# Relative attention: queries and keys loaded from GpSimd's queue, four places for raw rows, smaller groups of inverse roots at the end

## What is computed

```python
# first layer, per batch b and head h
srel = skew(einsum('bhnd,hmd->bhnm', qx, ex))          # row n moved by n places
qk   = (einsum('bhnd,bhmd->bhnm', qx, kx) + srel) / sqrt(8)
out  = softmax(qk - mask) @ vx ; x = layernorm(x + out @ Wp.T + bp)
# last layer, per token
y = sum over the two chosen experts of gate * gelu(h @ w1[e]) @ w2[e]
x = layernorm(x1 + y)
```

## Time and profile before

| | |
|---|---|
| median of 3 runs | 1973.78 us (1969.85 to 1980.45) |
| profiled execution | 1972.76 us, span 1971.0 us |
| busy share of the span | PE 87%, weight load 72%, DVE 70%, ACT 69%, POOL 50% |
| mean granted TensorE clock | 0.943 |
| attention of the first layer | from about 74 us to about 752 us |
| last layer's units, then the scatters that are left | to 1946 us, then to 1963.6 us |
| DMA | 349.7 MB, mean 177 GB/s; 1.54 MB in each quad's write and read |

### The profile page before, as it was taken

The page is one execution under the profiler, slowest core; times in us unless marked ns, Lnnn a source line. Parts: engine busy times, 40 slices in busy tenths (PEclk is TensorE's granted clock), DMA queues, the critical chain, the costliest instruction groups (busy, mean ns, idle before and its releaser), DMA issues. The chain is left out here.

```text
span 1971.0 us, 51107 instructions
## 1 busy us (share of the span) xinstructions
PE 1720.8 (87%) x15932; PEld 1410.7 (72%) x15932; DVE 1381.4 (70%) x5696; ACT 1368.5 (69%) x3385; POOL 978.2 (50%) x1256
## 2 busy tenths in 40 slices
PE   7799998999998998898999768898859999748994
PEld 6566665665655566788999758888748999727994
DVE  1388887887877785585432279999859888584663
ACT  3589988888888883423455458888849888515784
POOL 2133333333333333215667666666328989925755
PEclk9899999999999997999999979999979999857997
DMA  7899999999999994104566612222131212266852
GB/s 218 278 319 325 339 322 317 319 317 314 335 310 301 322 308 129 44 1 129 173 185 200 171 36 58 62 60 64 41 83 33 55 33 60 38 103 186 245 182 81
DMA packets 220349, 349.72 MB, mean 177 GB/s; under 512 B 55960, under 2 KB 167832, under 8 KB 219576
## 3 DMA queue, kind: packets, MB, share of 16 engines
q1 hardware_dynamic: 185096, 304.95, 48.9%
q0 software_dynamic: 14144, 31.16, 6.6%
q10 hardware_dynamic: 20848, 10.36, 1.8%
HBM read 160.52 MB, written 144.38 MB: 155 GB/s over the span
## 5 line engine op out<-in xcount | busy, mean ns | idle before, releaser
L184 POOL TENSOR_SCALAR_AFFINE_SELECT heads_raw_relative<-heads_raw_relative 128x508 f32<-128x508 f32 x256 | 158.8, 645 | 485.5 <-ACT heads_raw_relative L569 446.2
L575 ACT ACTIVATE attend_prob_t<-attend_turn_bank 128x384 f32<-128x384 f32 x512 | 225.3, 492 | 35.8 <-PE attend_turn_bank L493 34.5
L569 ACT COPY heads_raw_relative<-heads_rel_bank 128x768 f32<-128x768 f32 x247 | 198.0, 802 | 63.7 <-PE heads_rel_bank L464 30.9
L493 PE MATMUL attend_turn_bank<-ident,attend_score 128*128 128x128 f32 x1536 | 229.6, 285 | 5.4 <-ACT attend_prob_t L575 4.3
L493 PEld LDWEIGHTS attend_turn_bank<-ident,attend_score 128*128 128x128 f32 x1536 | 165.3, 142 | 94.4 <-ACT attend_prob_t L575 47.2
L628 DVE CUSTOM_DVE_ANT_0 attend_score<-attend_score_bank,heads_relative 128x128 f32<-128x128 f32 x512 | 146.1, 285 | 101.7 <-PE attend_score_bank L464 59.6
L631 DVE CUSTOM_DVE_ANT_0 attend_score<-attend_score_bank,heads_relative 128x256 f32<-128x256 f32 x512 | 214.5, 419 | 0.0
L637 DVE TENSOR_SCALAR attend_score<-attend_score,attend_extreme 128x256 f32<-128x256 f32 x512 | 187.5, 366 | 0.0
L579 ACT ACTIVATE attend_score<-attend_score,attend_extreme 128x128 f32<-128x128 f32 x512 | 181.7, 412 | 2.2 <-DVE attend_extreme L631 1.9
L1432 POOL DMA_INDIRECT moe_route_rows_sb<-tokens,moe_taken x154 | 145.7, 946 | 70.0 <-PE moe_route_bank L1459 41.3
L461 PE MATMUL heads_rel_bank<-heads_e,heads_qk 32*128 32x128 f32 x988 | 123.1, 325 | 52.5 <-ACT heads_raw_relative L569 32.6
(11 more groups left out here) (455 smaller groups left out, 5221.9 us busy)
## 6 DMA issues: line engine op xcount, KB each, us to landing
shear<-heads_raw_relative SPq DMA_DIRECT2D x128, 768.0 KB, 8.2
heads_relative<-shear SPq DMA_DIRECT2D x128, 768.0 KB, 6.6
duo_w_now<-moe_w SPq DMA_DIRECT2D x158, 129.0 KB
moe_route_w_now<-moe_w SPq DMA_DIRECT2D x154, 129.0 KB
expert_out<-moe_route_y ACTq DMA_DIRECT2D x38, 256.0 KB
qk_heads<-heads_qk_out SPq DMA_DIRECT2D x32, 256.0 KB, 3.9
heads_qk<-qk_heads SPq DMA_DIRECT2D x128, 64.0 KB
pair_rows<-groups SPq DMA_DIRECT2D x16, 260.0 KB, 7.5
```

Source lines behind the costliest of these rows:

```text
L184: m = nc.gpsimd.affine_select(out=future, in_=future, compare_op=ALU.is_ge, fill=-BIG, base=1 - P, pattern=[[0, QUAD], [1, P - 1]], channe ...
L493: mm = nc.tensor.transpose(bank[:, j * P:(j + 1) * P], score[:, (h - LAG) % RING, j * P:(j + 1) * P], c.ident[:, :])
L569: nc.scalar.copy(raw[:, ring, 2 * half:2 * half + 2, :], r_bank[:, :, 0:W]).then_inc(rel_moved, 1)
L575: nc.scalar.activation(prob_t[:, (h - LAG) % RING, :], bank_of(h)[:, 0:W], ACT.Exp).then_inc(exped, 1)
```

## The change

Three edits.

1. In the attention stage the loads of queries and keys of batch t + 2 leave SP's program and go to GpSimd's, one group of 8 partitions in each of steps 1 to 4. With them go the wait for VectorE's sums of batch t - 1 and, in the first batch, the wait for the projected rows. The two early loads of the project stage stay on SP's queue, on semaphores of their own, so that TensorE's count in step 7 is changed.
2. `raw` has four places in place of three.
3. In the last layer groups end at 8, 16, 24, 32, 40, 44, 48, 52, 56, 60, 62 and 64. From tile 40 on a root has three instructions in a unit (the last again all at once), and its tiles may be scaled from two units behind it on, not three.

```diff
@@ class Heads
-    SLOTS, AHEAD, RAWS, MV, STORES = 3, 9, 3, 32, 4
+    SLOTS, AHEAD, RAWS, MV, STORES = 3, 9, 4, 32, 4
...
-def load_heads(sp, c, heads, t, slot):
+def load_heads(engine, c, heads, t, slot, groups, done):
 
     rows = c.qk_heads[t]
-    for g in range(QUAD):
-        sp.dma_start(heads.qk[32 * g:32 * g + HD, slot, :, 1:], of_group(rows, g)).then_inc(heads.qk_in[slot], 16)
+    for g in groups:
+        engine.dma_start(heads.qk[32 * g:32 * g + HD, slot, :, 1:], of_group(rows, g)).then_inc(done, 16)
...
@@ attend_relative, SP's program
-                    if quad == 0 and t == 0:
-                        for r in range(heads_in.STORES):
-                            sp.wait_ge(heads_in.stored[r], 16 * B // heads_in.STORES)
-                    if quad == 0 and (t + 2 < B):
-                        wait_past(sp, summed, NH * t)
-                        load_heads(sp, c, heads_in, t + 2, (t + 2) % SLOTS)
@@ TensorE's program
-                                pe.wait_ge(qk_in[slot], 16 * QUAD * (more + 1))
+                                pe.wait_ge(qk_in[slot], 16 * QUAD * (more + (slot == 2)))
@@ GpSimd's program
                     if s == 1:
                         take_values(t, v)
+                    if s == 1 and t == 0:
+                        for r in range(heads_in.STORES):
+                            pool.wait_ge(heads_in.stored[r], 16 * B // heads_in.STORES)
+                    if 1 <= s <= QUAD and t + 2 < B:
+                        wait_past(pool, summed, NH * t)
+                        load_heads(pool, c, heads_in, t + 2, (t + 2) % SLOTS, (s - 1,), qk_in[(t + 2) % SLOTS])
                     if s == 4 and not first:
                         add_bias(t - 1)
@@ route_pairs
-    ends = list(range(8, NT - 16 + 1, 8)) + [NT - 8, NT - 4, NT]
+    ends = list(range(8, NT - 24 + 1, 8)) + list(range(NT - 20, NT - 3, 4)) + [NT - 2, NT]
...
-        return finished(ends[k] - 1) + 3 + j // (1 if k < len(ends) - 3 else 2 if k < len(ends) - 1 else ROOT_STEPS)
+        return finished(ends[k] - 1) + 3 + j // (1 if ends[k] < NT - 24 else 3 if ends[k] < NT else ROOT_STEPS)
...
-            soonest = max(root_at(k, ROOT_STEPS - 1) + 3, kept_at[-1] + 1 if t else 0)
+            soonest = max(root_at(k, ROOT_STEPS - 1) + (3 if ends[k] < NT - 24 else 2), kept_at[-1] + 1 if t else 0)
```

10 lines of the change are left out of this document (5 added, 5 removed).

## The result

The changed kernel takes 2048.53 us (median of 4 runs, 2042.02 to 2051.99) against 1974.8 us of the kernel before beside it: 1.0364 times as long, with an interval of 1.0334 to 1.0394. That is 74 us more, where 18 us less were forecast, and above the range (1938 to 1988). The profiled execution has a span of 2049.0 us where the one before had 1971.0, so 78.0 us are to be found in the trace.

What follows compares the result with a forecast made beforehand. The prediction took the engines' pace of 20.0 us a batch plus 27.2 us of stalls, from loads ahead of a write, as the bound. From 1972.8 us, -22 + 9 - 4.6 = -17.6 gave 1955.2, range 1938 to 1988.

Steps and rivals of the forecast that it cites:

- What bounds the kernel: Attention stage: engines' own pace is 20.0 us a batch; 27.2 us of stalls come in single batches.
- The loads leave SP's queue, -22: Attention, SP's queue: writes land 2.6 to 3.4 us sooner, most of 27.2 us of stalls go, 5 kept: -22 us.
- The fourth load, +9: Attention, TensorE's step 7: the load lands after 3.8 us where 3.5 are left, 0.3 us in 29 batches: +9 us.
- Rival A: Attention: the late fourth load makes TensorE wait in every batch; 1999 us at a landing of 5.5 us; chance 0.29.
- Four places, nothing: Places of `raw`: ScalarE's waits for one go, but VectorE waits as long for the read; costed at nothing.
- Tail, -4.6: Last layer's end: smaller groups let scatters run without a gap from tile 29 on: -4.6 us.
- GpSimd has room: Attention: GpSimd is busy 200 of 600 us; four issues of 0.95 us add 3.8 us to a 20 us batch.
- Rival B: Attention: same bytes on the same DMA engines, so stalls stay and only the end is shorter: 1968 us; chance 0.15.

Runs made afterwards that it cites:

- The tiny loads: Kernel before plus 120 loads of 512 bytes from GpSimd's queue, in steps 0 to 3 of batches 0 to 29, read by nothing: 1965.60 us against 1975.06.

## Why the prediction was wrong

**What bounds the kernel: right.** 20.0 us a batch as the engines' own pace, 27.2 us of stalls, and the loads ahead of the write as their cause. Runs without loads, or with the loads behind the write, have marks of 20.0.

**The loads leave SP's queue, -22: right, and small.** No stall of SP's is left in the changed kernel, and at full pace, with the loads sooner, the marks are 20.0: all 27.2 went, none of the 5 kept back stayed. The write landed 3.0 us sooner, inside the 2.6 to 3.4, but partly by luck: its batches are longer and their DMA share is 0.86; at a pace of 20.0 us it is 1.9 us (6.3). And the reason that the prediction leaned to, uneven engines that another queue's cursor would even out, was not needed: the same loads on SP's queue, behind the write, cure the stalls as well. What no run shows is which DMA engines carried what.

**The fourth load, +9: this is the step that failed.** Its place was right, and so was the time it has (3.5 us), the wait at L461 and its 29 repetitions. Its landing was taken as 3.8 us, from gathers of twice the size; it was 6.1 at the median (6.3 over all four) and 6.7 in the batch shown. Measured, the term is 69.3 + 27.2 = 96.5 us, 3.3 a batch: 2.6 us of wait, and 0.7 for the low clock after it, which 21 of the 29 batches have and which costs such a batch some 1.1 us beyond its wait. The range of landings that the prediction used (3.1 to 5.5) did not hold the value. Two things made the term too small. The bound went by single landings up to 5.5, at a DMA share of 0.24, and by 4.4 at 0.86; but the attention has 0.96, and its own reads of the earlier trace rows need 6.6. The prediction took those as too large an upper neighbour, since they have 12 times the bytes. The tiny loads show that the bytes hardly mattered: the nearest row by traffic was the read itself. Rival A was the right mechanism (a wait in every batch came; its nearly equal marks did not, they are 20.2 to 25.9) with a price too low at its far end (5.5, giving 1999); at 6.3 us its own formula gives 1941 + 2.8 x 29 = 2022. And the price of a wait was taken as its length, although already showed a clock of 0.50 behind one; that is 0.7 x 29 = 20 us more. Rival A with both sizes and the stage's end, 2022 + 20 + 9, comes to 2051, and the profiled execution took 2050.7; as the three sizes were measured in this very trace, that closes the sum and tests nothing. The test is the run with all four loads a step sooner. (A slip in the range of the forecast: a fourth load 0.7 us late gives 1941 + 0.7 x 29 = 1961, not 1963.)

The Trainium skill (DMA: Bandwidth & Descriptors, the section on the anatomy of one DMA on GpSimd's path) fits such a transfer as 2.0 us and its bytes by 436 GB/s, which is 2.2 us for 64 KB and 2.0 for 512 bytes. In this stage it was 6.3 to 7.3 for the one and 6.3 for the other: that they are nearly equal agrees, the level does not, so the fit is no price at the DMA shares of these runs (0.84 to 0.99).

**The end of the stage, 9.2 us: no term.** A barrier at the end of a stage was taken as untouched by the queue on which loads are issued. The trace before couldn't price it, but a sentence could have named it: GpSimd issued no transfer in this stage before.

**Four places, nothing: right.** With edit 1 alone the ratio is the same within its interval, and ScalarE waits for no place. **Tail, -4.6: right,** measured -4.4; between the run with edit 1 alone and the two others of its set with the new groups it is -3.4 and -2.3. VectorE's last unit came 3.4 us later after the stage's first gather (163.2 in place of 159.8), more than the 2.4 allowed for, and the rows were covered all the same.

**GpSimd has room: right**, with 0.56 us an issue instead of 0.95. But room was not the question; the landing was.

**Rival B: no.** The stalls went. Its rule in the Trainium skill (the same page, on issuing engines that are not separate DMA queues) would have warned against the change by another way: it says that moving transfers to another engine's queue gains only the time of the issue, and what cured the stalls was indeed order, to be had on SP's queue. And at a pace of 20.0 us the write lands after 6.3 us with the loads on GpSimd's queue and after 6.1 with them behind it on SP's, 8.2 before: the queue's own part is nothing that shows, and order on the one queue is worth more than the 1.76 us of issue.

What the forecast hoped for exists: 1972.8 - 31.8 = 1941 was its full gain, and the kernel with two and two loads behind the write on SP's queue takes 1943.77.

## What to carry to other kernels

A transfer that is moved needs its time from start to landing under the traffic of its new place; take it from a transfer that runs in that traffic, not from one of like size in a quiet stage, and put it against the moment its reader needs it. If the margin is unknown, start it as soon as its place is free: one step was worth 4.6% of the time here. Before moving loads to another queue, try to reorder the one they are in: what is waited for first goes first, what has a batch's time goes behind it. And a wait of TensorE can cost more than its length: here about 1.1 us more in the 21 batches of 29 in which the clock fell behind it.

## What was not expected of the hardware

- Loads from GpSimd's queue land after 6.3 to 7.3 us at the median in this attention with 64 KB (DMA shares of 0.84 to 0.99), and after 6.3 with 512 bytes; the last of three in a burst takes 8.7 at the median and up to 9.8.
- Whether four loads of 64 KB stand ahead of a write of 768 KB on SP's queue or, two and two, behind it changes that write's landing from 10.0 to 6.1 us with four places.
- A stage in which GpSimd's queue has loaded heads ends later, by 0.077 us for each such load (9.2 for 120, 6.9 for 88), whether the loads are long over or not; transfers of 512 bytes do not do it (0 for 120, 0.7 for 128). The cause stays open.
- Behind an idle time of 3.2 us the granted clock of TensorE is 0.50 to 0.54 for some 3 us. Not every such wait does it: behind 2.73 us in another batch it stays at 1.00.
